# Sixteen batches of graph attention and a routed expert layer on one core: the attention's instruction order on all four engines laid out anew

## Chip, cores and metric

One core of one Trainium2 chip runs the whole program. The metric is the device time in microseconds (us), the median of the runs shown. Engines: PE (TensorE), DVE (VectorE), ACT (ScalarE), POOL (GpSimd), SP (the DMA queue).

## What is computed

The input holds 16 batches of 256 tokens with 128 features. In each batch and each of 16 heads of 64 features:

```python
sim = einsum(q, k) * scale, causal mask;  attn = softmax(sim)
out = attn @ v
adj = clip(attn + eye, 0, 1);  deg = sum(adj)
feats = v
for l in range(2):
    h = feats @ gnn_w[l] + gnn_b[l]
    feats = gelu(adj @ h / deg + feats)
out = layer_norm((out + feats @ lin_w + lin_b) @ Wo)
x = x + out
# then a mixture of 8 experts, two for each token
logits = rmsnorm(layer_norm(x)) @ router;  top 2;  silu(gate) * up @ down
```

## The kernel before

Heads go in 8 pairs n (0 to 7), pairs in 4 doubles d. `queries_keys(b, n)` makes q and k of a pair with three float32r products each, `scores(b, n)` the 256x256 scores of two heads, `maxima` (DVE) and `exps` (ACT) their softmax numerator, `adjacency` (DVE) adds the diagonal and sums a row (`den`), `weights` takes its reciprocal, `graph` (POOL) scales the matrix, `transposes` (PE) turns it and `graph` (ACT) keeps it in SBUF as `gt0`, `gt1`. `differences` (PE) multiplies it by v into the half bank MIX, `degrees` (POOL, then PE) puts den/ssum, transposed, into the half DEG. `difference` (DVE) writes MIX - v to `dT`, `attended` multiplies it by DEG into `aT`. `mixed_values`, `layer1`, `layer2_in` and `layer2` are the graph layers of a double; `layer1_out` and `layer2_out` (DVE) and `gelu1` and `gelu2` (ACT) close them. `output_start`, `output_graph` and `output_attended` add up the output product of a batch in bank 7, `output_natural` turns it.

A tensor instruction uses one of three shapes of the array. Most are 128 rows by 128 columns. `scores` has 64 x 128 (two heads in two row halves). `differences` and `layer2` have 128 x 64 (two heads in two column halves). In the profile they stand as 128\*128, 64\*128 and 128\*64. A block is one call of such a function; a stretch of blocks with one shape is called a group below, and the passage from one group to the next a switch.

The four engines each run a list of calls written out by hand, `batch(b, before, routed, after)`: batches 0 and 1, then a loop over 2 to 14, then batch 15. The list mixes four batches: the attention of b, the rest of the output and norms of b-1, routing of b-2 (`logits`, `places`, `choose`, `place_tokens`, on POOL four `scatter` DMAs), and norm, values and first queries of b+1. Engines meet by counters: `Signal.wait(engine, turn, k)`. Each of the eight PSUM banks has fixed uses (`SCORE_BANKS`, `TURNED_BANKS`, bank 0 for `queries_keys` and `layer1`, 3 and 4 for `transposes`, 5 for MIX and DEG). Behind the batches stands the sorted stage: 71 steps of 128 routed rows, each loaded by DMA, multiplied and stored by an indirect DMA (`rows_out`).

Of the kernel before, what the change touches and what calls it, by code (L numbers as in the profile page):

```python
# [20 lines left out]
P = 128  # L21
BATCHES, TOKENS, DIM = 16, 256, 128
HEADS, DHEAD = 16, 64
# [42 lines left out]
class Signal:  # L66
# [5 lines left out]
    def wait(self, engine, turn, k):  # L72

        engine.wait_ge(self.sem, turn * self.per + k)


def build_program(nc, x, wq, wk, wv, wvT, gnn_w, gnn_b, lin_wT, lin_b, wo, gamma_in, gamma_out,
# [10 lines left out]
    with ctx:  # L88
# [10 lines left out]
        hold = sb("hold", [P, 2])  # L99
# [97 lines left out]
        dT = at("dT", [P, TOKENS])  # L197
# [68 lines left out]
        s_vt, a_vt = Signal(sem("s_vt"), 4), Signal(sem("a_vt"), 4)  # L266
        a_d = Signal(sem("a_d"), PAIRS)
# [47 lines left out]
        LOGITS, PLACES = slice(0, TILES * EXPERTS), slice(0, (SIDE + 1) * EXPERTS)  # L315
# [7 lines left out]
        VALUE_BANKS = (3, 4, 5, 3)  # L323
        L1_BANK, L2_IN_BANKS, L2_BANKS = 0, (2, 2, 2, 4), (1, 1, 1, 3)
        MIX, DEG = slice(0, TOKENS), slice(TOKENS, 2 * TOKENS)

        def score_bank(n, a):
            return bank[SCORE_BANKS[(2 * n + a) % 3]]

# [126 lines left out]
        def _(pool):  # L456
# [71 lines left out]
            def degrees(b, n):  # L528

                s = n % 3  # L530
                if n >= 3:
                    s_deg.wait(pool, b, n - 2)
# [9 lines left out]
            def scatter(p, c):  # L542

                nc.gpsimd.indirect_dma_start(slots, bass.IndirectOffsetOnAxis(ap=row_now[:, c:c + 1], axis=0),
                                             z4[:, c, :], None).then_inc(z_free.sem, 16)

# [16 lines left out]
            def batch(b, before, routed, after):  # L563

                if routed is not None:
                    gate_up_low(b - 1)
                graph(b, 0)
                graph(b, 1)
                degrees(b, 0)
                degrees(b, 1)  # L570
                graph(b, 2)
                degrees(b, 2)
                graph(b, 3)
                graph(b, 4)
                if after is not None:
                    deviation(after, 0, 3)
                if before is not None:
                    token_power(before, 0)
                degrees(b, 3)
                degrees(b, 4)  # L580
                if routed is not None:
                    d_pl.wait(pool, routed, 5)
                graph(b, 5)
                if routed is not None:
                    for c in range(SIDE):
                        scatter(routed, c)
                degrees(b, 5)
                graph(b, 6)
                degrees(b, 6)
                graph(b, 7)  # L590
                degrees(b, 7)
                if after is not None:
                    deviation(after, 1, 7)
                if before is not None:
                    token_power(before, 1)
# [11 lines left out]
            batch(0, None, None, 1)  # L607
            p_deg.wait(pool, 0, PAIRS)
# [36 lines left out]
        def _(pe):  # L645
# [30 lines left out]
            def x_transposed(b, earlier):  # L676
                d_ln.wait(pe, b, 8)
                if earlier is not None:
                    a_exp.wait(pe, earlier, 2 * PAIRS - 1)
                for t in range(TILES):  # L680
                    mm = nc.tensor.transpose(bank[6][:, xt(t)], xh[:, t, :], ident[:, :])
                mm.then_inc(s_xt.sem, 1)

            def values(b, c, earlier):

                t, h = c % 2, c // 2
                if c == 0:
                    a_xt.wait(pe, b, 1)
                    d_xt.wait(pe, b, 1)
                    if earlier is None:  # L690
                        pe.wait_ge(k_vlow, 2)
                    else:
                        a_gt.wait(pe, earlier, PAIRS)
                        d_z2.wait(pe, earlier, DOUBLES)
                if c == 1 and earlier is not None:
                    a_gt.wait(pe, earlier, PAIRS)
                    a_g1.wait(pe, earlier, DOUBLES)
                if c == 2 and earlier is not None:
                    a_d.wait(pe, earlier, PAIRS)
                if c == 3:  # L700
                    a_v.wait(pe, b, 1)
                cols = slice(h * 512, (h + 1) * 512)
                product3(bank[VALUE_BANKS[c]][:, :], xt_hi[:, xt(t)], xt_lo[:, xt(t)],
                         v_hi[:, cols], v_lo[:, cols]).then_inc(s_v.sem, 1)

            def queries_keys(b, n, earlier=None):
                if n == 0:
                    if earlier is not None:
                        d_z1.wait(pe, earlier, DOUBLES)
                    a_xt.wait(pe, b, 1)  # L710
                    d_xt.wait(pe, b, 1)
                else:
                    a_qk.wait(pe, b, n)
                cols = slice(n * P, (n + 1) * P)
                product3(bank[0][:, 0:TOKENS], w_hi[:, 0, cols], w_lo[:, 0, cols], xt_hi[:, :], xt_lo[:, :])
                product3(bank[0][:, TOKENS:], w_hi[:, 1, cols], w_lo[:, 1, cols],
                         xt_hi[:, :], xt_lo[:, :]).then_inc(s_qk.sem, 1)

            def scores(b, n, before=None, routed=None):

                a_qk.wait(pe, b, n + 1)
                if n == 0 and before is not None:
                    d_z2.wait(pe, before, DOUBLES)
                    a_g1.wait(pe, before, DOUBLES)
                if n == 1 and routed is not None:
                    d_ch.wait(pe, routed, 1)
                if n >= 1:
                    a_exp.wait(pe, b, 2 * n - 1)
                q, k = qk[:, n % 2, 0:TOKENS], qk[:, n % 2, TOKENS:]
                for h in range(2):  # L730
                    for a in range(2):
                        rows = slice(a * DHEAD, (a + 1) * DHEAD)
                        diagonal = score_bank(n, a)[:, :].rearrange("p (t j) -> p t j", t=TILES)
# [9 lines left out]
            def values_transposed(b, i):  # L743

                a_v.wait(pe, b, (2, 3, 4, 4)[i])
                if i == 3:
                    a_vt.wait(pe, b, 1)
                o = bank[TURNED_BANKS[i]]
# [7 lines left out]
            def transposes(b, n):  # L756
# [3 lines left out]
                if n >= 1:  # L760
                    a_gt.wait(pe, b, n)
                else:
                    a_vt.wait(pe, b, 4)
                for a in range(2):
                    nc.tensor.transpose(bank[3][:, a * TOKENS:a * TOKENS + P], ea[:, s, a, :], ident[:, :])  # L765
                    nc.tensor.transpose(bank[3][:, a * TOKENS + P:(a + 1) * TOKENS], eb[:, s, a, 0:P], ident[:, :])  # L766
                for a in range(2):
                    mm = nc.tensor.transpose(bank[4][:, a * P:(a + 1) * P], eb[:, s, a, P:], ident[:, :])  # L768
# [11 lines left out]
            def differences(b, n):  # L780

                a_gt.wait(pe, b, n + 1)
                if n >= 1:
                    a_d.wait(pe, b, n)
                mixed(bank[5][:, MIX], lambda t, a: vnat[:, t, n * P + a * DHEAD:n * P + (a + 1) * DHEAD], n)

            def degrees(b, n):

                p_deg.wait(pe, b, n + 1)
                for t in range(TILES):  # L790
                    mm = nc.tensor.transpose(  # L791
                        bank[5][:, DEG][:, xt(t)],
# [3 lines left out]
            def output_natural(b):  # L796

                d_yT.wait(pe, b, 1)
                for t in range(TILES):
                    mm = nc.tensor.transpose(bank[7][:, xt(t)], yT[:, xt(t)], ident[:, :])  # L800
                mm.then_inc(s_yn.sem, 1)

            def layer1(b, d):
# [3 lines left out]
                if d == 0:  # L807
                    a_qk.wait(pe, b, PAIRS)
                else:
# [1283 lines left out]
```

## Time and profile before

| | |
|---|---|
| median of 3 runs | 1095.57 us (1093.75 to 1097.4) |
| profiled execution, span | 1095.5 us |
| PE busy | 1058.7 us, 97% |
| DVE busy | 861.7 us, 79% |
| ACT busy | 783.5 us, 72% |
| POOL busy | 503.4 us, 46% |
| mean granted PE clock | 0.998 |
| chain that ended last | PE 62%, DVE 26%, issue 5%, ACT 2%, DMA 2% |

The profiled execution has no time of its own beside its span of 1095.5 us; it lies 0.1 us from the median. Times are from the span's start. PE busy is a modelled number: matmuls are pipelined, so an engine that reads 97% busy can still lose time between one matmul's start and the next. In the timeline a row merges neighbouring instructions, the second number is its length, and starts can be compared from row to row.

### The profile page before, as it was taken

Reading aid. Unit: us, or ns where it says so; the run is one execution under the profiler, and the core shown is the slowest. Engines: PE = TensorE matmul, PEld = TensorE weight load, DVE = VectorE, ACT = ScalarE, POOL = GpSimd, SP = SyncE. Lnnn points to the kernel's source line nnn. Section 1 sums busy time; section 2 is a strip of 40 time slices with the busy share of each in tenths; the row PEclk is TensorE's granted clock in tenths of the full one; section 3 lists DMA queues with packets and bytes.
Section 4 is the critical chain, followed back from the end, with each engine's and each line's share of the span. In section 5 each row is a group of like instructions: output and inputs, shape, how many; then the busy total and the mean of one; then the engine's idle time right before and its main releaser. Section 6 shows DMA issues by size and latency. Waiting matters only on the chain.

```text
span 1095.5 us, 28320 instructions
## 1 busy us (share of the span) xinstructions
PE 1058.7 (97%) x8600; PEld 857.1 (78%) x8600; DVE 861.7 (79%) x3622; ACT 783.5 (72%) x2180; POOL 503.4 (46%) x654
## 2 busy tenths in 40 slices
PE   5999999999999999999999999999999989999997
PEld 4777777777777777777777777778787767999995
DVE  5758797979798888979797979797979696767554
ACT  5768686868686868686878777778687776656653
POOL 4515254544545453536363626272727251655443
PEclk9999999999999999999999999999999999999999
DMA  6990000000000000000000000000000012222227
GB/s 179 404 328 2 9 2 19 0 18 0 11 7 10 8 10 8 10 8 10 8 10 8 10 8 10 8 10 8 10 8 10 1 38 73 62 65 74 62 60 243
DMA packets 48965, 50.04 MB, mean 46 GB/s; under 512 B 20601, under 2 KB 39291, under 8 KB 48912
## 3 DMA queue, kind: packets, MB, share of 16 engines
q1 hardware_dynamic: 44592, 40.91, 12.2%
q0 software_dynamic: 4320, 8.47, 2.3%
q8 instruction: 28, 0.46, 0.2%
q14 instruction: 25, 0.20, 0.1%
HBM read 21.23 MB, written 28.58 MB: 45 GB/s over the span
## 4 chain that ended last, share of the span: by engine, by line
PE 62%; DVE 26%; issue 5%; ACT 2%; DMA 2%; SPq 2%; POOL 0%; DVEq 0%; POOLq 0%
PE bank L648 51%; DVE eb L1478 6%; DVE nmax L1463 6%; DVE ea L1475 3%; PE bank L791 2%; PE bank L1023 2%; DVE dT L1492 1%; PE bank L765 1%; PE bank L752 1%; PE bank L766 1%; PE bank L768 1%; DVE aT L1497 1%; ACT f1T L1186 1%; DVE z L1512 1%; DMA pairs<-zout,zin 1%
## 5 line engine op out<-in xcount | busy, mean ns | idle before, releaser
L522 POOL TENSOR_TENSOR ea<-ea,wgt 128x256 f32<-128x256 f32 x128 | 78.3, 611 | 308.9 <-DVE wgt L1487 289.3
L1463 DVE TENSOR_REDUCE nmax<-bank 128x1 f32<-128x128 f32 (+1 forms) x512 | 149.3, 346 | 67.0 <-PE bank L648 67.0
L1128 ACT ACTIVATE gt<-bank 128x512 f32<-128x512 f32 (+1 forms) x256 | 111.8, 494 | 41.0 <-PE bank L768 40.2
L1160 ACT ACTIVATE ea<-bank,nmax 128x128 f32<-128x128 f32 x256 | 96.5, 377 | 52.2 <-DVE nmax L1463 29.5
L524 POOL TENSOR_TENSOR eb<-eb,wgt 128x512 f32<-128x512 f32 x128 | 132.7, 1037 | 0.0
L1478 DVE SCALAR_TENSOR_TENSOR eb<-idw,ssum,eb 128x256 f32<-128x256 f32 x256 | 126.2, 530 | 0.0
L1160 ACT ACTIVATE eb<-bank,nmax 128x256 f32<-128x256 f32 x256 | 123.8, 484 | 0.0
L648 PE MATMUL bank<-gt,vnat 128*64 128x256 f32 (+1 forms) x1024 | 111.2, 336 | 11.3 <-ACT gvT L1128 10.5
L648 PEld LDWEIGHTS bank<-gt,vnat 128*64 128x64 f32 x1024 | 68.3, 136 | 56.8 <-issue 35.4
L648 PE MATMUL bank<-qk 64*128 64x128 f32 (+1 forms) x1024 | 112.7, 340 | 0.0
L550 POOL DMA_INDIRECT pairs<-zout,zin x71 | 70.7, 996 | 80.7 <-DVE zout L1983 68.0
L648 PE MATMUL bank<-gt,g 128*64 128x256 f32 (+1 forms) x1024 | 97.0, 330 | 1.0
L648 PE MATMUL bank<-xt_lo,w_hi 128*128 128x256 f32 x256 | 88.3, 345 | 2.3 <-DVE xt_lo L1456 1.9
L648 PEld LDWEIGHTS bank<-gt,g 128*64 128x64 f32 x1024 | 68.5, 137 | 27.3 <-issue 9.5
L1128 ACT ACTIVATE qk<-bank 128x512 f32<-128x512 f32 x128 | 76.8, 600 | 15.3 <-PE bank L648 15.3
L540 POOL TENSOR_TENSOR rs<-ve,half 128x2 f32<-128x2 f32 x48 | 34.4, 716 | 113.1 <-DVE ve L1742 58.8
L533 POOL TENSOR_TENSOR deg<-den,rs 128x256 f32<-128x256 f32 x128 | 82.3, 652 | 0.3
L1186 ACT ACTIVATE f1T<-z,gb 128x512 f32<-128x512 f32 x64 | 46.2, 722 | 48.1 <-DVE z L1512 47.9
L1520 DVE TENSOR_TENSOR z<-bank,f1T 128x512 f32<-128x512 f32 x64 | 44.0, 688 | 46.4 <-PE bank L648 46.3
L1475 DVE SCALAR_TENSOR_TENSOR ea<-ident,ssum,ea 128x128 f32<-128x128 f32 x256 | 79.3, 347 | 0.0
L648 PE MATMUL bank<-aT,wo_sb 128*128 128x256 f32 x256 | 78.1, 388 | 0.0
L1976 DVE TENSOR_TENSOR shid<-bank,ssg 128x352 f32<-128x352 f32 x71 | 37.3, 525 | 50.9 <-ACT ssg L1323 43.4
(240 smaller groups left out, 3102.4 us busy)
## 6 DMA issues: line engine op xcount, KB each, us to landing
slots<-gu_lo SPq DMA_DIRECT2D x33, 520.0 KB, 14.9
zin<-slots SPq DMA_DIRECT2D x71, 65.0 KB, 1.8
got<-pairs SPq DMA_DIRECT2D x8, 512.0 KB, 6.8
zin<-in_guT SPq DMA_DIRECT2D x14, 216.0 KB, 2.9
raw_gu<-in_guT SPq DMA_DIRECT2D x8, 352.0 KB, 4.0
out<-x_all SPq DMA_DIRECT2D x7, 256.0 KB, 3.0
pairs<-zout,zin POOLq DMA_INDIRECT x71, 2.6
dn<-in_downT SPq DMA_DIRECT2D x2, 512.0 KB, 15.6
```

What stands on the lines that cost most here:

```text
L522: nc.gpsimd.tensor_tensor(ea[:, s], ea[:, s], wgt[:, s, 0:2].unsqueeze(2).to_broadcast([P, 2, P]), ALU.mult)
L524: nc.gpsimd.tensor_tensor(eb[:, s], eb[:, s], wgt[:, s, 2:4].unsqueeze(2).to_broadcast([P, 2, 2 * P]), ALU.mult).then_inc(p_g.sem, 1)
L533: nc.gpsimd.tensor_tensor(deg[:, s], den[:, s, :].unsqueeze(2).to_broadcast([P, 4, DHEAD]), rs[:, s, :].unsqueeze(2).to_broadcast([P, 4, D ...
L550: nc.gpsimd.indirect_dma_start(pairs, bass.IndirectOffsetOnAxis(ap=zin[:, j % RING, ID:ID + 1].bitcast(u32), axis=0), zout[:, j % RING, :] ...
L648: return nc_mm(o, st, mo, start=first, stop=last, **more)
L1128: return nc.scalar.activation(o, i, ACT.Copy, **more)
L1160: done = nc.scalar.activation(e[:, s, a, :], score_bank(n, a)[:, TILE_SCORES[t]], ACT.Exp, bias=nmax[:, s, i:i + 1], accum_out=ssum[:, s, ...
L1186: nc.scalar.activation(f1T[:, d % 2, :], z1[:, d % 2, :], ACT.Gelu, bias=gb[:, 0:1]).then_inc(a_f1.sem, 1)
L1463: done = V.tensor_reduce(nmax[:, n % 3, i:i + 1], score_bank(n, a)[:, TILE_SCORES[t]], X, ALU.max, negate=True)
L1475: V.scalar_tensor_tensor(ea[:, s, a, :], ident[:, :], ssum[:, s, a:a + 1], ea[:, s, a, :], ALU.mult, ALU.max, accum_out=den[:, s, a:a + 1])
L1478: done = V.scalar_tensor_tensor(eb[:, s, a, :], idw[:, :], ssum[:, s, 2 + a:3 + a], eb[:, s, a, :], ALU.mult, ALU.max, accum_out=den[:, s, ...
L1520: V.tensor_tensor(z2[:, d % 2, :], bank[L2_BANKS[d]][:, :], f1T[:, d % 2, :], ALU.add).then_inc(d_z2.sem, 1)
```

## The change

Nothing of the computation changes. All four lists are written in another order. On PE: `scores` of pairs 0 and 1, 2 and 3, 4 and 5 stand together, `differences` 2 and 3 too, `differences` 6 behind `layer2(0)`, `layer2` 2 and 3 together. Every use of PSUM has its bank from a table, so that neighbouring blocks write different banks. Waits inside the functions are gone where the order of the lists or one wait in `batch` covers them. `difference` writes `MIX - v` straight to `aT` and `attended` multiplies `aT` in place; `difference` waits for `differences` alone (new signal `s_d`), no longer for `degrees`. One product, `output_attended(b, 3)`, moves to the next batch. On POOL the four scatters move from the middle of the list to its end.

```diff
-        SCORE_BANKS = (1, 2, 6)
-        TURNED_BANKS = (4, 5, 3, 4)
+        SCORE_BANKS = ((1, 5), (4, 6), (3, 2), (0, 5), (3, 0), (5, 4), (6, 5), (6, 3))
+        QK_AT = ((3, 0), (3, 0), (2, 0), (0, 0), (4, 0), (0, 0), (1, 0), (4, 0))
...
             def difference(b, n):
 
-                s_deg.wait(dve, b, n + 1)
-                V.tensor_tensor(dT[:, :], bank[5][:, MIX], vT[:, n, :], ALU.subtract).then_inc(d_d.sem, 1)
+                s_d.wait(dve, b, n + 1)
+                V.tensor_tensor(aT[:, n, :], psum(MIX_AT[n], TOKENS), vT[:, n, :], ALU.subtract).then_inc(d_d.sem, 1)
 
             def attended(b, n):
 
                 d_d.wait(dve, b, n + 1)
-                V.tensor_tensor(aT[:, n, :], bank[5][:, DEG], dT[:, :], ALU.mult).then_inc(d_a.sem, 1)
+                V.tensor_tensor(aT[:, n, :], psum(DEG_AT[n], TOKENS), aT[:, n, :], ALU.mult).then_inc(d_a.sem, 1)
...
             def adjacency(b, n):
 
                 s = n % 3
                 a_exp.wait(dve, b, 2 * n + 2)
-                if n >= 3:
-                    p_deg.wait(dve, b, n - 2)
...
 # POOL, batch()
+                if before is not None:
+                    token_power(b - 1, 0)
+                if routed is not None:
+                    scatters(b - 2)
+                if before is not None:
+                    token_power(b - 1, 1)
                 if routed is not None:
                     z_free.wait(pool, routed, z_free.per)
                 if before is not None:
-                    token_power(before, 2)
+                    token_power(b - 1, 2)
...
 # PE, batch(), beginning and end
-                scores(b, 0, before)
-                queries_keys(b, 2)
-                if routed is not None:
-                    logits(routed, bank[6])
-                values(b, 1, before)
-                values(b, 2, before)
-                scores(b, 1, None, routed)
+                a_v.wait(pe, b, 1)
+                scores(b, 0)
+                d_z2.wait(pe, b - 1, 3)
+                scores(b, 1)
+                a_zt.wait(pe, b - 2, 1)
+                queries_keys(b, 2)
...
+                a_exp.wait(pe, b, 5)
+                values_transposed(b, 0)
+                transposes(b, 0)
...
+                layer2_in(b, 3)
+                layer2(b, 2)
+                layer2(b, 3)
                 output_graph(b, 2)
-                layer2(b, 2)
-                layer2_in(b, 3)
-                if after is not None:
-                    queries_keys(after, 0, b)
-                if before is not None:
-                    tokens_transposed(before, bank[6], after)
-                layer2(b, 3)
...
 # DVE, batch(), middle
                 maxima(b, 5, 1)
+                p_deg.wait(dve, b, 2)
                 adjacency(b, 4)
-                difference(b, 1)
-                weights(b, 4)
+                if before is not None:
+                    output_bias(b - 1)
...
+                difference(b, 1)
+                maxima(b, 6, 0)
+                weights(b, 4)
+                p_deg.wait(dve, b, 3)
+                adjacency(b, 5)
+                maxima(b, 6, 1)
```

The beginning of the loop's list on PE, before. `mask,pick` and `qk` are `scores`, `xt_lo,w_hi` to `xt_hi,w_hi` are `queries_keys`.

```order
L648 MATMUL bank<-mask,pick 128x2x64 x4
L648 MATMUL bank<-qk 128x128 x2
L648 MATMUL bank<-qk 128x256 x2
L74 REGISTER_ALU
L648 MATMUL bank<-xt_lo,w_hi 128x256
L648 MATMUL bank<-xt_hi,w_lo 128x256
```

The same place in the changed kernel.

```order
L665 MATMUL bank<-mask,pick 128x2x64 x4
L665 MATMUL bank<-qk 128x128 x2
L665 MATMUL bank<-qk 128x256 x2
L76 ISA
L76 REGISTER_ALU
L665 MATMUL bank<-mask,pick 128x2x64 x4
L665 MATMUL bank<-qk 128x128 x2
L665 MATMUL bank<-qk 128x256 x2
L665 MATMUL bank<-xt_lo,w_hi 128x256
```

The scores of pair 1 now follow those of pair 0 directly; before, fourteen matmul calls on the full array stood between them.

The end of the loop's list on PE, before, from `tokens_transposed` on (`gt,g` is `layer2`, `f2T,lwo` is `output_graph`).

```order
L970 MATMUL bank<-ident,z 128x128 x2
L648 MATMUL bank<-gt,g 64x256 x2
L648 MATMUL bank<-gt,g 64x128 x2
L648 MATMUL bank<-gt,g 64x256 x2
L648 MATMUL bank<-gt,g 64x128 x2
L74 REGISTER_ALU
L648 MATMUL bank<-xt_lo,w_hi 128x256
```

And in the changed kernel, from `layer2_in(b, 3)` (`gw,f1T`) on.

```order
L665 MATMUL bank<-gw,f1T 128x128 x4
L665 MATMUL bank<-gt,g 64x256 x2
L665 MATMUL bank<-gt,g 64x128 x2
L665 MATMUL bank<-gt,g 64x256 x2
L665 MATMUL bank<-gt,g 64x128 x2
L665 MATMUL bank<-gt,g 64x256 x2
L665 MATMUL bank<-gt,g 64x128 x2
L665 MATMUL bank<-gt,g 64x256 x2
L665 MATMUL bank<-gt,g 64x128 x2
L665 MATMUL bank<-f2T,lwo 128x256
L76 ISA
L974 MATMUL bank<-ident,z 128x128 x2
```

`layer2` of the last two doubles is now one group, and the queries and values of the next batch stand ahead of it.

The loop's list on POOL around the scatters (`slots<-z,row_now`), before.

```order
L522 TENSOR_TENSOR ea<-ea,wgt 128x256
L524 TENSOR_TENSOR eb<-eb,wgt 128x512
L544 DMA slots<-z,row_now 33792x130 x4
L533 TENSOR_TENSOR deg<-den,rs 128x256
L74 REGISTER_ALU
```

And in the changed kernel, at the list's end (`rs<-ve,half` is `token_power`).

```order
L544 TENSOR_TENSOR deg<-den,rs 128x256
L76 ISA
L551 TENSOR_TENSOR rs<-ve,half 128x2
L76 ISA
L561 TENSOR_TENSOR hold<-half 128x1
L555 DMA slots<-z,row_now 33792x130 x4
L76 REGISTER_ALU
L551 TENSOR_TENSOR rs<-ve,half 128x2
```

The scatters now stand behind all eight `graph` and `degrees` of the batch and ahead of two `token_power`.

## Rows read from the trace of the kernel before

**Rows 1.** Page, part 1 (busy) and one group of part 5 (copies of ACT).

```profile
PE 1058.7 (97%) x8600; PEld 857.1 (78%) x8600; DVE 861.7 (79%) x3622; ACT 783.5 (72%) x2180; POOL 503.4 (46%) x654
...
L1128 ACT ACTIVATE qk<-bank 128x512 f32<-128x512 f32 x128 | 76.8, 600 | 15.3 <-PE bank L648 15.3
```

**Rows 2.** Busy time of one loop batch: window, length, PE, PEld, DVE, ACT, POOL, clock, DMA.

```profile
458.10:514.37 56.27, 55.41 (x465) 43.59 (x463) 47.52 (x212) 42.51 (x122) 26.53 (x34) 1.00 0.03 9
```

**Rows 3.** Timeline of PE: start, length, instructions; `transposes` of x for the next batch.

```profile
458.10 0.44 PE L681 MATMUL bank<-ident,xh 128*128 128x128 f32 x2
...
514.37 0.44 PE L681 MATMUL bank<-ident,xh 128*128 128x128 f32 x2
```

**Rows 4.** Timeline of PE in that batch, blocks inside a group and beside a switch.

```profile
495.86 0.38 PE L791 MATMUL bank<-ident,deg 128*128 128x128 f32 x2
496.07 0.27 PE L765 MATMUL bank<-ident,ea 128*128 128x128 f32 x1
...
496.73 0.60 PE L648 MATMUL bank<-aT,wo_sb 128*128 128x256 f32 x2
...
500.68 0.27 PE L765 MATMUL bank<-ident,ea 128*128 128x128 f32 x1
...
501.43 0.87 PE L648 MATMUL bank<-gt,vnat 128*64 128x256 f32 x8
502.23 0.44 PE L791 MATMUL bank<-ident,deg 128*128 128x128 f32 x2
502.51 1.03 PE L648 MATMUL bank<-gvT,gw 128*128 128x256 f32 x4
...
504.60 0.87 PE L648 MATMUL bank<-gt,vnat 128*64 128x256 f32 x8 [0.17 <-ACT gvT L1128]
505.27 1.50 PE L648 MATMUL bank<-gt,g 128*64 128x256 f32 x16
```

**Rows 5.** Timeline of PE, `differences(2)` and what it waited for.

```profile
494.59 0.87 PE L648 MATMUL bank<-gt,vnat 128*64 128x256 f32 x8 [0.38 <-ACT gvT L1128]
```

**Rows 6.** Timeline of PE, start of a batch: `scores(0)`, `queries_keys(2)`, `logits`, then `values(1)`.

```profile
469.12 0.29 PE L648 MATMUL bank<-mask,pick 64*128 64x128 bf16 x4
...
470.05 0.38 PE L648 MATMUL bank<-xt_lo,w_hi 128*128 128x256 f32 x1
...
470.84 0.51 PE L648 MATMUL bank<-rtT,zT 128*128 128x8 f32 x4
471.20 0.48 PE L648 MATMUL bank<-v_lo,xt_hi 128*128 128x512 f32 x1
```

**Rows 7.** Timeline of ACT, `exps(3, 0)` and the start of `exps(3, 1)`.

```profile
482.90 0.38 ACT L1160 ACTIVATE ea<-bank,nmax 128x128 f32<-128x128 f32 x1
...
483.71 0.38 ACT L1160 ACTIVATE ea<-bank,nmax 128x128 f32<-128x128 f32 x1
```

**Rows 8.** Timeline of POOL, first scatter of a batch, what follows the fourth, and one `token_power`.

```profile
500.51 1.06 POOL L544 DMA_INDIRECT slots<-z,row_now  x1 [0.17 <-issue]
...
505.56 0.73 POOL L533 TENSOR_TENSOR deg<-den,rs 128x256 f32<-128x256 f32 x1
...
514.87 0.69 POOL L540 TENSOR_TENSOR rs<-ve,half 128x2 f32<-128x2 f32 x1 [3.35 <-DVE ve L1692]
```

**Rows 9.** Timeline of DVE, one instruction of `adjacency` at two places.

```profile
484.68 0.48 DVE L1478 SCALAR_TENSOR_TENSOR eb<-idw,ssum,eb 128x256 f32<-128x256 f32 x1
...
900.20 1.82 DVE L1478 SCALAR_TENSOR_TENSOR eb<-idw,ssum,eb 128x256 f32<-128x256 f32 x1
```

**Rows 10.** Timeline of POOL beside the last of them.

```profile
900.71 1.03 POOL L524 TENSOR_TENSOR eb<-eb,wgt 128x512 f32<-128x512 f32 x1
```

**Rows 11.** Timeline of PE, `tokens_transposed` in loop and last batch, last `transposes` of x.

```profile
465.33 0.38 PE L970 MATMUL bank<-ident,z 128*128 128x128 f32 x2
...
851.96 0.44 PE L681 MATMUL bank<-ident,xh 128*128 128x128 f32 x2
...
920.29 0.44 PE L970 MATMUL bank<-ident,z 128*128 128x128 f32 x2 [0.38 <-DVE z L1752]
```

More of the change, by code:

```diff
@@ L918, in batch @@
-                degrees(b, 2)
-                transposes(b, 4)
-                output_attended(b, 0)
-                scores(b, 7)
-                differences(b, 3)
-                degrees(b, 3)
-                layer1(b, 0)
-                output_attended(b, 1)
+                    output_attended(b - 1, 6)
+                a_exp.wait(pe, b, 9)
+                transposes(b, 2)
+                a_qk.wait(pe, b, 7)
+                degrees(b, 1)
+                if before is not None:
+                    output_attended(b - 1, 7)
+                    output_graph(b - 1, 7)
@@ new lines, in batch @@
+                degrees(b, 2)
+                degrees(b, 3)
+                differences(b, 2)
+                differences(b, 3)
+                d_y.wait(pe, b - 1, 1)
+                scores(b, 7)
+                a_d.wait(pe, b, 2)
+                transposes(b, 4)
+                output_attended(b, 1)
+                output_attended(b, 2)
+                a_exp.wait(pe, b, 14)
+                layer1(b, 0)
+                a_gt.wait(pe, b, 5)
+                degrees(b, 4)
+                values_transposed(b, 2)
@@ L939, in batch @@
-                degrees(b, 6)
-                transposes(b, 7)
+                degrees(b, 7)
+                if after is not None:
+                    x_transposed(b + 1)
+                differences(b, 7)
+                d_z1.wait(pe, b, 3)
                 layer2(b, 1)
-                differences(b, 7)
                 if after is not None:
-                    x_transposed(after, b)
-                degrees(b, 7)
+                    a_d.wait(pe, b, 7)
+                    queries_keys(b + 1, 0)
@@ L946, in batch @@
                 output_graph(b, 0)
+                layer1(b, 3)
+                layer2_in(b, 2)
+                if after is not None:
+                    a_qk.wait(pe, b + 1, 1)
+                    queries_keys(b + 1, 1)
+                    d_z2.wait(pe, b, 2)
+                    values(b + 1, 0)
                 output_graph(b, 1)
-                output_attended(b, 3)
-                layer2_in(b, 2)
-                layer1(b, 3)
+                layer2_in(b, 3)
+                layer2(b, 2)
@@ new lines, in batch @@
+                weights(b, 6)
+                if before is not None:
+                    norm_tokens(b - 1, 0)
+                a_vt.wait(dve, b, 3)
+                difference(b, 4)
+                layer1_out(b, 1)
+                attended(b, 4)
+                adjacency(b, 7)
+                if routed is not None:
+                    choose(b - 2, 2)
+                weights(b, 7)
+                difference(b, 5)
+                if routed is not None:
+                    place_tokens(b - 2, 0)
@@ L1593, in batch @@
+                attended(b, 5)
+                layer2_out(b, 0)
+                difference(b, 6)
+                if before is not None:
+                    norm_tokens(b - 1, 1)
+                attended(b, 6)
+                if after is not None:
+                    norm_step(b + 1, 5)
+                if routed is not None:
+                    place_tokens(b - 2, 1)
+                layer1_out(b, 2)
                 if after is None:
                     table_first(0)
+                if before is not None:
+                    norm_tokens(b - 1, 2)
@@ L1608, in batch @@
[L1608 to L1616 removed]
+                    x_low(b + 1)
+                if before is not None:
+                    norm_tokens(b - 1, 3)
+                attended(b, 7)
```

554 lines of the change are left out of this document (246 added, 308 removed).

## The prediction

> **What bounds the kernel now.** I read the busy shares first. PE is busy for 97% of the span, DVE for 79%, ACT for 72%, POOL for 46% [rows 1]. Only something that makes PE's own list shorter can give much. Next comes the window of one loop batch, from one `transposes` of x to the next, 514.37 - 458.10 = 56.27 us [rows 3]. In it PE is busy 55.41 us, so its idle time is 0.86 us, while DVE has 47.52 and ACT 42.51 [rows 2]. Sixteen such batches are some 900 us of the span; the sorted stage behind them is not touched.
>
> Then I ask what the busy time consists of, and here the length of a row says less than the distance between starts. The same block takes different times by what stands beside it [rows 4]. `transposes` with full-array work on both sides takes 496.73 - 496.07 = 0.66 us; with `differences` behind it, which uses 128\*64, it takes 501.43 - 500.68 = 0.75. `differences` takes 502.23 - 501.43 = 0.80 us when the full array comes next, but 505.27 - 504.60 = 0.67 when `layer2` follows, which has its own shape. `degrees` takes 0.21 us (495.86 to 496.07) behind full-array work and 502.51 - 502.23 = 0.28 behind `differences`. So PE loses time where the array's shape changes: 0.09 or 0.13 us at the end of the block before, and 0.07 at the start of the block behind.
>
> **The change, part by part.**
>
> *Switches.* I counted the groups in the two lists for a loop batch. Before there are 33 switches: each of the 8 `scores` and most of the 8 `differences` and 4 `layer2` stand alone. In the changed list there are 21. Scores 0 and 1, 2 and 3, 4 and 5 take away two each, differences 2 and 3, differences 6 behind `layer2(0)`, and `layer2` 2 and 3 two each: 12. By the rows of the last paragraph one switch costs between 0.09 (nothing at the entry) and 0.20 us (0.13 + 0.07). I take 0.14: the exit of 0.09 plus a part of the entry, since the entry is seen on small blocks and large ones may hide it. That is 12 x 0.14 = 1.68 us in each batch, with 1.1 and 2.4 as ends. It lies wholly on PE, which nothing hides.
>
> *Waits of PE.* The loop batch has 0.86 us of idle time [rows 2]. One part is `differences(2)`, which waited 0.38 us for the one MIX bank to be copied by `mixed_values(1)` [rows 5]. With banks from tables this cause is gone. What comes next? I checked the new order at three places by adding up blocks.
>
> At the beginning, PE reaches `values_transposed(0)` after 4 scores, 3 `queries_keys`, `logits`, a `values` and four products of the output. `scores` is 0.93 us, `queries_keys` 0.79, `logits` 0.36 [rows 6]; with some 0.8 for `values` and 0.4 for each output product (estimates: as many columns as `queries_keys`, and half of it) this is 3.7 + 2.4 + 0.4 + 0.8 + 1.7 = 9.0 us, less 0.2 for the switches gone, 8.8 us. It now waits for `exps(2, 0)`. On ACT five `exps` at 483.71 - 482.90 = 0.81 us [rows 7] and three copies of 0.6 [rows 1] stand ahead of its end, 5.9 us, and they can begin when the first scores (0.93 us) and their `maxima` (some 0.6 us, an estimate) are through: 7.4 us. About 1.4 us are left, which waits on the way may use up.
>
> At the end, POOL has the four scatters ahead of the last two `token_power`. They take 505.56 - 500.51 = 5.05 us, a `token_power` 0.69 [rows 8]. DVE's `norm_tokens(7)` waits for the second power and `norm_tokens(11)` for the third, and `layer2_out(2)` and `layer2_out(3)` are queued behind them. From `place_tokens(1)` on this chain is 5.05 + 0.7, then four norm steps and a power, about 2.6, then two more DVE steps of about 0.7 each: 9.8 us. In the same time PE has from `x_transposed` to the next batch's second scores 13 us of work by the same block sums: 4 blocks of `layer2` of 1.4 us and half, two `queries_keys`, `values`, two `layer2_in`, `layer1`, three output products, the first scores. Some 3 us of cover: I cost the move of the scatters at nothing. If the cover were gone, `scores(1)` would be late first.
>
> In the middle the matter is DVE. At 47.5 us of work in 54.6 it is 87% used, against 84% before, and between `adjacency(2)` and `layer1_out(0)` it hardly rests. `attended(2)` must be through before PE's `output_attended(2)`, and `layer1_out(0)` before `degrees(5)`. My additions leave next to no slack there. So I don't count the 0.38 us as won, nor any of the 0.86: I put the idle time after equal to that before. The ends are 0 (a gain of 0.9) and 2.5 us.
>
> *In place and fewer waits.* `difference` and `attended` stay two DVE instructions of the same size; one reads SBUF where it read `dT`, nothing gained. `difference` can begin before `degrees`: this only gives DVE freedom. The counters that go are checks without work; PE's list has fewer, and I cost them at nothing: where a count had long been reached, the rows show the next block starting without a gap. `output_attended(b, 3)` is only moved. Batches 0, 1 and 15 use the same lists, so the switches go there too.
>
> *Batch 15.* In the loop `tokens_transposed` starts 465.33 - 458.10 = 7.2 us after a window opens [rows 3, 11]. The last of those windows opens at 851.96, so it would end 56.27 us later at 908.23, and the start would be at 908.23 + 7.2 = 915.5; it was at 920.29, 4.8 us late [rows 3, 11], although PE has fewer blocks there. Eight `gate_up_high` on ACT and `table_first` on DVE stand in the way. The new list spreads them singly; it may give 3 us or take 2. I leave it at 0.
>
> **Sum.** The profiled span is 1095.5 us, 0.1 from the median of 1095.57, so it can stand for it. 16 x 1.68 = 26.9 us: 1095.5 - 26.9 = 1068.6, **1069 us**. A batch should take 54.6 us.
>
> **The other ways.**
>
> *Waits shrink too.* If the spread banks remove nearly all idle time and a switch is worth more than 0.14, a batch is 53.7 us: 16 x 2.6 = 41, giving 1054. For it: the waits now are for single banks [rows 5]. Against: DVE's load in the middle.
>
> *DVE and POOL in each other's way, part of the gain lost.* An `adjacency` instruction of 0.48 us took 1.82 us at 900.20 [rows 9], while POOL ran its `graph` instruction from 900.71 on [rows 10]. The two were in each other's way. The Trainium skill, SBUF — State Buffer, section Who interferes with whom, says that a VectorE instruction with two inputs in SBUF contends with a GpSimd instruction that reads SBUF; the trace agrees at this place. In the new order `adjacency` 4 to 7 fall in the stretches in which POOL does `graph` and two `degrees` in a row, since these now follow each other without scatters between. If half of the 16 large and small instructions of these four are held for 0.3 us, the middle is 2.4 us later than in my sum, and after the little slack some 1 us of it stays as waits of PE: 16 x (1.68 - 1) = 11, giving 1085.
>
> *The same, and slower than before.* All 16 held, some by 1.3 us as at 900.20, is 16 x 0.3 + 1.3 = 6 us of delay a batch, of which 3 us can't be caught up: the batch is 54.6 + 3.0 = 57.6 us and the time 1095.5 + 16 x 1.3 = 1116. The place is `output_attended(2)`, `layer1(0)` and `degrees(5)` on PE; the point from which it decides is 1.7 us more waiting in a batch than now, since PE is the bound and never wins back what it waited.
>
> *The saving is not there.* The price of a switch might be a drain that has to come anyway before the next block's results are used, then 12 fewer change nothing: 1095. Against it: 0.67 and 0.80 us for the same eight instructions.
>
> **Chances.** Forecast 1069 with its neighbours (1062 to 1078): 0.5. Waits shrink: 0.18. Part lost, about 1085: 0.17. No saving: 0.05. Slower, about 1116: 0.10. A measurement of this kernel can tell 0.3%, some 3 us, from no change. Faster is then 0.5 + 0.18 + 0.16 = 0.84, within 0.3% 0.05, slower 0.11. The range reaches from 1054, the better end of the waits, to 1088, the partial loss with its spread, and leaves out some 2 in 10.
>
> **What would show it.** The distance between two starts of `transposes` of x in the loop: 54.6 us; 53.7 or 55.6 for the two neighbours. 21 switches in a batch; a block of `scores` that follows another starts some 0.1 us sooner behind it than 0.93. PE's idle time in the window near 0.9 us. If the batch is longer than 55.5, the waits list must name DVE (`aT`, `z`) or ACT behind DVE as releaser, and `adjacency` instructions of more than 0.5 us must be many in the middle. If `layer2_out(2)` is late behind `norm_tokens(7)`, the scatters were not covered. The forecast is wrong in its ground if the loop batch has 12 switches fewer and is not shorter although PE doesn't wait.

## The result, and the profile after

The changed kernel takes 1054.45 us, the median of four runs between 1054.06 and 1054.87. The kernel before took 1096.49 beside it, the median of four runs between 1093.75 and 1098.01. The ratio is 0.9623, with a 95% interval from 0.9607 to 0.9638: faster by 42 us, where 27 was forecast. That is the lower end of the range, and the time that the rival "waits shrink too" gave (1054, with a loop batch of 53.7 us; it came out at 53.5).

The page of the changed kernel, whose profiled span is 1053.1 us; the first line is its part 1, to be held against [rows 1], the second its part 4, the shares of the chain of waits that ended last.

```profile
PE 1022.9 (97%) x8600; PEld 855.3 (81%) x8600; DVE 856.3 (81%) x3622; ACT 777.8 (74%) x2180; POOL 505.3 (48%) x668
...
PE 78%; DVE 11%; ACT 3%; issue 3%; DMA 2%; SPq 2%; POOL 0%; POOLq 0%; DVEq 0%; ACTq 0%
```

PE is still busy for 97% of the span, and the span is 42.4 us shorter: what became shorter is PE's own busy time. The window of one loop batch, between two `transposes` of x (us of the window, then the busy time and instructions of PE, PE's weight loads, DVE, ACT and POOL, then the granted clock):

```profile
544.66:598.14 53.48, 53.12 (x465) 43.52 (x464) 47.23 (x210) 42.07 (x122) 26.59 (x35) 1.00 0.03 9
```

Against [rows 2] the window went from 56.27 to 53.48 us and PE's busy time from 55.41 to 53.12, with the same 465 matmul records. Counted in the traces from the array shape of each record, a batch has 21 switches where it had 33. Idle time is 0.36 where it was 0.86. All the waiting of PE that the rows show is now in one place, at `scores(7)`. Rows of PE's timeline (start, length, engine, line, operation):

```profile
544.65 0.38 PE L696 MATMUL bank<-ident,xh 128*128 128x128 f32 x2
...
556.91 0.28 PE L665 MATMUL bank<-mask,pick 64*128 64x128 bf16 x4
...
557.74 0.28 PE L665 MATMUL bank<-mask,pick 64*128 64x128 bf16 x4
...
583.34 0.29 PE L665 MATMUL bank<-mask,pick 64*128 64x128 bf16 x4 [0.36 <-DVE y_now L1502]
...
598.13 0.38 PE L696 MATMUL bank<-ident,xh 128*128 128x128 f32 x2
```

The reader is to see two things. `scores(1)` starts 557.74 - 556.91 = 0.83 us behind `scores(0)`, where a block of scores that had the full array behind it took 0.93 [rows 6]. And `scores(7)` waits for `y_now`, which `output_kept` on DVE copies out of the bank in which the scores go. By the starts on either side this wait is 0.43 us (0.36 in the row), so a batch that doesn't wait there would take 53.48 - 0.43 = 53.04 us (unrounded starts). That number is the yardstick below.

Where the 42.4 us of the two spans came from, by the starts of `transposes` of x: the start -0.1 (its end came 0.1 later); batch 0 0.3 (55.55 to 55.28); batch 1 3.5 (55.99 to 52.53); thirteen batches of 2.79, 36.3; batch 15 2.6; the sorted stage nothing (172.9 and 173.0). For batch 15, the first row is the first product of the sorted stage in the kernel before, the others are the end of batch 15 in the changed one.

```profile
922.64 0.27 PE L1005 MATMUL bank<-ident,zin 128*128 128x128 f32 x1
```

```profile
875.01 1.16 PE L665 MATMUL bank<-gw,f1T 128*128 128x128 f32 x8 [1.56 <-ACT f1T L1182]
...
879.46 0.38 PE L974 MATMUL bank<-ident,z 128*128 128x128 f32 x2
...
880.12 0.27 PE L1007 MATMUL bank<-ident,zin 128*128 128x128 f32 x1
```

From the last `transposes` of x (851.96 [rows 11], and 812.03 now) to this product it is 70.68 us before and 68.09 now, although a wait of 1.56 us for ACT stands in it.

The contention that the prediction feared is there. DVE's timeline around `adjacency(5)`, and POOL's for the same stretch:

```profile
472.48 0.31 DVE L1472 SCALAR_TENSOR_TENSOR ea<-ident,ssum,ea 128x128 f32<-128x128 f32 x1
...
472.73 0.69 DVE L1472 SCALAR_TENSOR_TENSOR ea<-ident,ssum,ea 128x128 f32<-128x128 f32 x1
...
473.35 1.25 DVE L1475 SCALAR_TENSOR_TENSOR eb<-idw,ssum,eb 128x256 f32<-128x256 f32 x1
...
474.53 0.82 DVE L1475 SCALAR_TENSOR_TENSOR eb<-idw,ssum,eb 128x256 f32<-128x256 f32 x1
...
475.82 0.41 DVE L1502 COPY y_now<-bank 128x256 f32<-128x256 f32 x1
```

```profile
472.57 0.70 POOL L535 TENSOR_TENSOR ea<-ea,wgt 128x256 f32<-128x256 f32 x1 [2.39 <-DVE wgt L1484]
473.23 1.09 POOL L537 TENSOR_TENSOR eb<-eb,wgt 128x512 f32<-128x512 f32 x1
474.28 0.79 POOL L544 TENSOR_TENSOR deg<-den,rs 128x256 f32<-128x256 f32 x1
```

`weights(4)` on DVE releases POOL's `graph(4)` and `degrees(4)` just as DVE begins `adjacency(5)`. The large instruction that takes 0.48 us alone [rows 9] takes 1.25 and 0.82 here, and the block is through after 2.9 us. In a whole batch 6 of the 32 instructions of `adjacency` are longer than their like (2 before), and this block has 3 of them. `y_now`, the copy for which PE waits, comes right behind it.

The scatters' move. POOL's rows and DVE's at the end of a batch:

```profile
491.59 1.06 POOL L555 DMA_INDIRECT slots<-z,row_now  x1 [0.16 <-issue]
...
496.45 0.73 POOL L551 TENSOR_TENSOR rs<-ve,half 128x2 f32<-128x2 f32 x1
```

```profile
497.22 0.60 DVE L1697 TENSOR_SCALAR t<-x_all,mv,rs 128x128 f32 x2 [0.65 <-POOL rs L551]
...
499.72 0.61 DVE L1748 TENSOR_SCALAR z<-t,rs 128x256 f32<-128x256 f32 x2 [0.80 <-POOL rs L551]
...
500.96 0.69 DVE L1513 TENSOR_TENSOR z<-bank,f1T 128x512 f32<-128x512 f32 x1 [0.48 <-PE bank L665]
```

DVE does wait for the powers behind the scatters, 0.65 and 0.80 us, and then `layer2_out(2)` still has to wait 0.48 us for PE. The move is covered.

### The profile page after: what moved, and what is told of

Read it like the earlier page. It is cut to its first block, busy times and chain, and to the rows that moved or that the text cites. A ratio compares the mean times of both kernels' runs of the same rounds, so it can differ in the third digit from the quotient of the medians.

```text
span 1053.1 us, 27818 instructions
## 1 busy us (share of the span) xinstructions
PE 1022.9 (97%) x8600; PEld 855.3 (81%) x8600; DVE 856.3 (81%) x3622; ACT 777.8 (74%) x2180; POOL 505.3 (48%) x668
## 4 chain that ended last, share of the span: by engine, by line
PE 78%; DVE 11%; ACT 3%; issue 3%; DMA 2%; SPq 2%; POOL 0%; POOLq 0%; DVEq 0%; ACTq 0%
PE bank L665 65%; DVE eb L1475 4%; DVE ea L1472 3%; PE bank L742 2%; PE bank L752 2%; PE bank L1025 2%; PE bank L753 2%; PE bank L755 2%; DVE nmax L1462 2%; PE bank L777 2%; ACT ea L1159 1%; ACT eb L1159 1%; DMA pairs<-zout,zin 1%; PE bank L1007 1%; DVE y_now L1502 1%
## 5 line engine op out<-in xcount | busy, mean ns | idle before, releaser
L1475 DVE SCALAR_TENSOR_TENSOR eb<-idw,ssum,eb 128x256 f32<-128x256 f32 x256 | 136.9, 570 | 0.0
L665 PE MATMUL bank<-gt,vnat 128*64 128x256 f32 (+1 forms) x1024 | 107.2, 335 | 0.4 <-ACT gt L1129 0.4
L665 PE MATMUL bank<-gt,g 128*64 128x256 f32 (+1 forms) x1024 | 92.2, 327 | 0.3 <-ACT g L1129 0.3
L665 PEld LDWEIGHTS bank<-gt,vnat 128*64 128x64 f32 x1024 | 63.2, 136 | 35.6 <-issue 16.0
L1129 ACT ACTIVATE gvT<-bank 128x256 f32<-128x256 f32 x128 | 49.9, 390 | 55.8 <-DVE aT L1494 55.7
L1472 DVE SCALAR_TENSOR_TENSOR ea<-ident,ssum,ea 128x128 f32<-128x128 f32 x256 | 90.9, 391 | 0.0
L665 PEld LDWEIGHTS bank<-gt,g 128*64 128x64 f32 x1024 | 65.4, 137 | 21.0 <-ACT g L1129 0.7
L665 PE MATMUL bank<-f2T,lwo 128*128 128x256 f32 x256 | 77.7, 386 | 0.3 <-ACT f2T L1192 0.3
L665 PE MATMUL bank<-aT,wo_sb 128*128 128x256 f32 x256 | 73.7, 391 | 0.0
L665 PE MATMUL bank<-xt_hi,w_hi 128*128 128x256 f32 x256 | 72.5, 283 | 0.0
```

Of the source, the lines that this page charges most:

```text
L665: return nc_mm(o, st, mo, start=first, stop=last, **more)
L1129: return nc.scalar.activation(o, i, ACT.Copy, **more)
L1472: V.scalar_tensor_tensor(ea[:, s, a, :], ident[:, :], ssum[:, s, a:a + 1], ea[:, s, a, :], ALU.mult, ALU.max, accum_out=den[:, s, a:a + 1])
L1475: done = V.scalar_tensor_tensor(eb[:, s, a, :], idw[:, :], ssum[:, s, 2 + a:3 + a], eb[:, s, a, :], ALU.mult, ALU.max, accum_out=den[:, s, ...
```

## The experiments

Two theories at the start: the gain is the price of the switches (A), or it comes mostly from shorter waits that the new order and its banks allow (B). Three kernels put switches back without moving anything far: one puts back six, one two, and a control makes a neighbour's move of the same kind without a switch more.

**Six switches back.** On PE:

```diff
                 scores(b, 2)
-                scores(b, 3)
                 if before is not None:
                     output_attended(b - 1, 3)
+                scores(b, 3)
+                if before is not None:
                     output_attended(b - 1, 4)
...
                 scores(b, 4)
-                a_gt.wait(pe, b, 2)
-                scores(b, 5)
                 if before is not None:
                     output_attended(b - 1, 5)
+                a_gt.wait(pe, b, 2)
+                scores(b, 5)
...
                 degrees(b, 2)
-                degrees(b, 3)
                 differences(b, 2)
+                degrees(b, 3)
                 differences(b, 3)
```

> The changed kernel with one full-array block set back between scores 2 and 3, between scores 4 and 5 and between differences 2 and 3: 27 switches in a loop batch where it has 21, the same blocks otherwise. Theory A (a switch costs PE 0.14 to 0.20 us): the loop batch goes from 53.5 to 54.3 to 54.7 us, the whole by 13 to 19 us. Theory B (the gain came from shorter waits alone, a switch costs nothing): 53.5 us, no change.

It took 1063.77 us (1062.34 to 1065.66), ratio 0.9701 [0.9682, 0.9720] to the kernel before. PE's timeline:

```profile
549.58 0.38 PE L696 MATMUL bank<-ident,xh 128*128 128x128 f32 x2
...
588.78 0.29 PE L665 MATMUL bank<-mask,pick 64*128 64x128 bf16 x4
...
603.58 0.38 PE L696 MATMUL bank<-ident,xh 128*128 128x128 f32 x2
```

A batch has 27 switches and takes 54.00 us, and `scores(7)` (the middle row) shows no wait: PE comes later, so `y_now` is there. Six switches therefore cost 54.00 - 53.04 = 0.96 us at most, 0.16 each; by the starts 0.05 of it is still waiting at `scores(7)`, which leaves 0.15 each. The saved wait hides some 0.4 of it. That put the batch under the 54.3 to 54.7 that A had named.

**Two switches back.** The second of the three hunks alone, `output_attended(5)` between scores 4 and 5.

```diff
                 scores(b, 4)
-                a_gt.wait(pe, b, 2)
-                scores(b, 5)
                 if before is not None:
                     output_attended(b - 1, 5)
+                a_gt.wait(pe, b, 2)
+                scores(b, 5)
```

> Only the block between scores 4 and 5 is set back: 23 switches. Theory A: one third of what the six cost, 0.28 to 0.40 us in a batch (53.75 to 53.87). Theory B: 53.47, no change.

**The control.** `output_attended(5)` behind `queries_keys(6)` instead; 21 switches as before.

```diff
                 scores(b, 5)
+                queries_keys(b, 6)
                 if before is not None:
                     output_attended(b - 1, 5)
-                queries_keys(b, 6)
```

> The same product as in the run with two more switches is moved past queries_keys(6), inside its group: 21 switches as before. Theory A: 53.5 us within 0.1. If it moves by more, then the moved product and not the switch explains part of the run with two.

The waits at `scores(7)`, first with two switches more, then the control:

```profile
586.11 0.29 PE L665 MATMUL bank<-mask,pick 64*128 64x128 bf16 x4 [0.28 <-DVE y_now L1502]
```

```profile
582.02 0.29 PE L665 MATMUL bank<-mask,pick 64*128 64x128 bf16 x4 [0.21 <-DVE y_now L1502]
```

With two switches more the batch takes 53.70 us with 0.34 of waiting by the starts, so 53.35 without: 0.31 above 53.04 (unrounded), 0.155 for a switch. The control takes 53.32 with 0.28 of waiting, again 53.04 without. One run each took 1059.42 and 1055.89 us. The control's batch is 0.16 us shorter than the changed kernel's, outside the 0.1 that was expected, and all of that is waiting. So this move of a block costs nothing by itself, and a switch costs 0.15 to 0.16 us at these places.

**All switches and all waits, by the starts.** The switches put back are not the twelve that the change took away, so their price can't simply be multiplied by 12. The traces settle it. Rows of PE in the kernel before, to be read with [rows 4] and [rows 5]:

```profile
486.30 0.70 PE L648 MATMUL bank<-aT,wo_sb 128*128 128x256 f32 x2
486.84 0.38 PE L791 MATMUL bank<-ident,deg 128*128 128x128 f32 x2
...
497.26 0.28 PE L648 MATMUL bank<-mask,pick 64*128 64x128 bf16 x4
...
500.25 0.60 PE L648 MATMUL bank<-aT,wo_sb 128*128 128x256 f32 x2
...
506.70 0.44 PE L791 MATMUL bank<-ident,deg 128*128 128x128 f32 x2
507.26 1.16 PE L648 MATMUL bank<-gw,f1T 128*128 128x128 f32 x8
```

`output_attended` takes 500.68 - 500.25 = 0.43 us with no switch beside it, 497.26 - 496.73 = 0.53 ahead of one and 486.84 - 486.30 = 0.54 behind one. Read so for every block, from the starts of its single matmuls, the exit costs 0.09 to 0.10 us (0.07 once) whatever the block. The entry costs 0.10 in the full-array products, 0.06 in transposes, 0.05 in `differences` and `layer2`, and 0.01 in `scores`. Summed over one loop batch, 33 switches are 4.9 us before and 21 are 3.2 now: the twelve that went are worth 1.68 us, 0.14 each. The six put back come to 0.91 by the same prices, 0.15 each.

The same starts give the waits. Before there are 1.7 us of them in a batch: 0.45 and 0.24 at the two `differences` that wait for the MIX bank, 0.38 at `layer1` behind `degrees` (507.26 - 506.70 = 0.56 where 0.28 is usual beside a switch [rows 4], and its first product is 0.1 late), and four of 0.11 to 0.24. All of these are gone. Two new ones have come, 0.43 at `scores(7)` and 0.15 at `transposes(7)`, together 0.58. That is 1.1 us less waiting, and 1.7 + 1.1 make up the 2.79. So theory A holds for 60% of the gain and theory B for 40%.

**One MIX bank's wait back.** To see what the tables of banks are worth for MIX, `differences(n)` waits again until `mixed_values(n - 1)` has copied, as with the single bank of before. On PE:

```diff
+                if n >= 1:
+                    a_d.wait(pe, b, n)
```

> The changed kernel with the old wait of a single MIX bank put back: differences(n) waits until mixed_values(n-1) has copied its half bank; order and banks stay. Theory A (the spread banks took the waits away, so putting the wait back brings back what the old kernel waited): the loop batch grows by 0.4 to 0.9 us. Theory B (the new order alone would have kept the wait short): below 0.1 us.

Both theories were far off. It took 1207.54 us (1205.71 to 1208.75), ratio 1.1021 [1.1000, 1.1041]. Window and PE's rows:

```profile
510.10:573.40 63.30, 55.61 (x464) 45.01 (x463) 47.11 (x209) 42.16 (x122) 26.75 (x36) 0.95 0.03 8
```

```profile
551.14 1.55 PE L665 MATMUL bank<-gt,vnat 128*64 128x256 f32 x8 [2.57 <-ACT gvT L1131]
554.42 1.55 PE L665 MATMUL bank<-gt,vnat 128*64 128x256 f32 x8 [1.73 <-ACT gvT L1131]
```

This batch is 63.3 us, 9.8 more than 53.48 (batches of 62.7 and 63.4 us take turns). A wait of one block cost 0.38 us in the old order, where other blocks stood between two differences [rows 5]. With them side by side it is a round trip from PE over DVE to ACT and back, 2.57 us at the longest, five waits and 7.7 us in a batch. The granted clock in the window is 0.95 where it was 1.00, with this much idle time, and PE's busy time is 55.61 us where it was 53.12. So for MIX the banks are not a gain beside the order: the new order can't be had without them. The other banks of the tables were not tried one by one.

**The differences not in place.** The tile `dT` comes back, and with it the wait that one tile needs:

```diff
+                if n >= 1:
+                    d_a.wait(dve, b, n)
-                V.tensor_tensor(aT[:, n, :], psum(MIX_AT[n], TOKENS), vT[:, n, :], ALU.subtract).then_inc(d_d.sem, 1)
+                V.tensor_tensor(dT[:, :], psum(MIX_AT[n], TOKENS), vT[:, n, :], ALU.subtract).then_inc(d_d.sem, 1)
...
-                V.tensor_tensor(aT[:, n, :], psum(DEG_AT[n], TOKENS), aT[:, n, :], ALU.mult).then_inc(d_a.sem, 1)
+                V.tensor_tensor(aT[:, n, :], psum(DEG_AT[n], TOKENS), dT[:, :], ALU.mult).then_inc(d_a.sem, 1)
```

> The changed kernel with differences written to their own tile dT again and, since one tile serves all pairs, DVE waiting for attended(n-1) before difference(n). Theory A (in place is worth nothing by itself, the sizes are the same and the wait is for an instruction that DVE has long done): the batch stays within 0.1 us of 53.47. Theory B (the wait of DVE on itself costs in the middle, where DVE has no slack): it grows by 0.2 to 0.5 us.

The batch is 53.57 us, 0.10 more, and one run took 1058.28. That difference of the totals is near what one run can tell, but the period of the batch is the same from batch to batch within 0.02, so the 0.10 stands; by the starts it is waiting at `transposes(7)`, where 0.15 had stood already. Computing in place is worth next to nothing, as costed.

**Is there slack on DVE in the middle?** The four reductions of `maxima(4)` are done twice, the second time into a spare tile: 1.06 us more on DVE.

```diff
+                if n in TWICE:
+                    for t in range(TILES):
+                        at_ = 4 * (n - 4) + 2 * t + a
+                        V.tensor_reduce(spare[:, at_:at_ + 1], score_bank(n, a)[:, TILE_SCORES[t]], X, ALU.max)
```

> The changed kernel with the four reductions of maxima(4) done twice, the copies into a spare tile: 1.06 us more work for DVE ahead of the middle of a batch. Theory A (as the prediction had it, DVE has next to no slack there): the batch grows by 0.8 to 1.1 us. Theory B (the new order has slack): below 0.4 us.

```profile
498.54 0.38 PE L698 MATMUL bank<-ident,xh 128*128 128x128 f32 x2
...
538.12 0.29 PE L667 MATMUL bank<-mask,pick 64*128 64x128 bf16 x4 [0.88 <-DVE y_now L1508]
...
552.93 0.38 PE L698 MATMUL bank<-ident,xh 128*128 128x128 f32 x2
```

The batch takes 54.39 us, 0.91 more for 1.06 us added, and one run took 1070.09. The wait at `scores(7)` (the middle row) grew by 0.5, and by the starts PE now also waits 0.3 to 0.4 at `output_start`, which needs `yT` from DVE. In the middle of a batch, work of DVE is on the path, although DVE is busy in only 47 of 53 us.

**What covers the scatters?** Four powers into a spare tile stand ahead of them on POOL.

```diff
+                for c in range(3, 7):
+                    nc.gpsimd.tensor_tensor(hold[:, c:c + 1], inv_e[:, 0:1], inv_e[:, 1:2], ALU.pow)
```

> The changed kernel with four powers of one column, some 2.8 us in all, ahead of the four scatters on POOL. Theory A (the prediction's block sums: 3 us of PE work cover the scatters): the batch stays within 0.2 us. Theory B (norm_tokens(7) and (11) already wait 0.65 and 0.80 us for POOL and layer2_out(2) stands behind them, so the cover is near 1.5 us): the batch grows by 1.0 to 1.5 us.

```profile
546.96 2.16 POOL L563 TENSOR_TENSOR hold<-inv_e 128x1 f32<-128x1 f32 x4
```

2.16 us more on POOL cost 0.31 us in a batch (53.78), one run 1061.30. That lies between the two theories. The slack behind the scatters was thus some 1.85 us (an estimate: 2.16 less 0.31), not the 3 of the prediction, and not nothing. By the starts PE becomes late at `values(1)` and `values(2)`, not at `scores(1)`, where the prediction looked for it.

**Taking the last wait away, first way.** On DVE `output_kept` is put ahead of `maxima(6, 1)`; on PE the control's move is kept.

```diff
                 adjacency(b, 5)
-                maxima(b, 6, 1)
                 if before is not None:
                     output_kept(b - 1, psum(Y_NOW_AT, TOKENS))
+                maxima(b, 6, 1)
```

> The changed kernel with output_kept of the batch before put ahead of maxima(6, 1) on DVE, and output_attended(5) behind queries_keys(6) on PE. scores(7) waits 0.43 us in each batch for output_kept. Theory A (this is the one wait that PE has left in a loop batch, and nothing else becomes late): the batch goes from 53.47 to 53.04 us and the whole by some 6 us, to about 1048. Theory B (exps(6, 1), now 0.33 us later, or another chain is late instead): 53.3 or more.

1050.19 us (1049.79 to 1052.45), ratio 0.9586 [0.9569, 0.9603], batch 53.21. The wait for `y_now` is gone, but the one near the end of the batch, where `transposes(7)` stands behind a wait for DVE's `layer2_out(0)`, has grown from 0.15 to 0.30 us by the starts. Of the 0.43 us, 0.27 were won and the rest was only put off, a result between the two theories.

**Second way: take away the cause.** On DVE `weights(4)` goes behind `adjacency(5)`, so that POOL gets its `graph(4)` when DVE is past those instructions.

```diff
-                weights(b, 4)
...
                 adjacency(b, 5)
+                weights(b, 4)
```

Timed once:

> The changed kernel with weights(4) put behind adjacency(5) on DVE, so that POOL's graph(4) no longer runs beside adjacency(5), which took 2.94 us in place of 1.43. Theory A (it is POOL's reading that holds these instructions): adjacency(5) takes 1.5 us, output_kept comes over 1 us earlier, the wait of scores(7) goes, the batch takes 53.1 us. Theory B (adjacency is long for another reason, or graph(4) is then late for transposes(4)): no shorter than 53.4.

It took 1047.71 us with a batch of 52.98. Then five times:

> The kernel with weights(4) behind adjacency(5) again, now timed against the kernel before over five rounds. From its loop batch of 52.98 us, 0.49 less than the changed kernel's, and some 15 batches: 7 us under the changed kernel's 1054.5, so 1047 to 1048; a ratio to the kernel before of 0.955 to 0.957.

1047.87 us (1046.58 to 1048.49), ratio 0.9555 [0.9542, 0.9568]: **this beats both kernels**, the changed one by 0.6%. PE's, then DVE's rows for `adjacency(5)`, then the group of the large instruction in the whole kernel, which is to be held against the last fence, of the changed kernel:

```profile
487.30 0.38 PE L696 MATMUL bank<-ident,xh 128*128 128x128 f32 x2
...
540.30 0.38 PE L696 MATMUL bank<-ident,xh 128*128 128x128 f32 x2
```

```profile
522.04 0.32 DVE L1472 SCALAR_TENSOR_TENSOR ea<-ident,ssum,ea 128x128 f32<-128x128 f32 x1
...
522.56 0.47 DVE L1475 SCALAR_TENSOR_TENSOR eb<-idw,ssum,eb 128x256 f32<-128x256 f32 x1
...
522.97 0.47 DVE L1475 SCALAR_TENSOR_TENSOR eb<-idw,ssum,eb 128x256 f32<-128x256 f32 x1
...
523.37 0.17 DVE L1484 RECIPROCAL wgt<-den 128x4 f32<-128x4 f32 x1
...
523.97 0.41 DVE L1502 COPY y_now<-bank 128x256 f32<-128x256 f32 x1
```

```profile
L1475 DVE SCALAR_TENSOR_TENSOR eb<-idw,ssum,eb 128x256 f32<-128x256 f32 x256 | 113.9, 481 | 0.0
```

```profile
L1475 DVE SCALAR_TENSOR_TENSOR eb<-idw,ssum,eb 128x256 f32<-128x256 f32 x256 | 136.9, 570 | 0.0
```

The large instructions are back at 0.47 us, and the mean over all 256 fell from 570 to 481 ns. `adjacency(5)` takes 1.3 us where it took 2.9, `y_now` is there in time, and the batch is 53.00 us, at the 53.04 that was worked out for a batch that doesn't wait at `scores(7)`. In the window PE is now busy in all of it; by the starts 0.1 us of waiting is left, at `transposes(7)`. The instructions are the same and as many; only what POOL did beside them was moved. So this wait came from the two engines being in each other's way, and not from too much work on DVE.

## Why the prediction was right and wrong

**The ground was right.** PE was the bound and stayed it; the larger part of the gain is 12 switches fewer in a batch, 33 to 21, and shows in PE's busy time. The sorted stage didn't move.

**The term of the switch was right in size.** "0.14: the exit of 0.09 plus a part of the entry" is what the twelve cost by the starts, 1.68 us in all. The reason given for it, that large blocks may hide the entry, is half right: `scores` hides it (0.01) and `differences` half of it (0.05), but the large products of the full array pay more than the small blocks, 0.10. That these balance to 0.14 is in part luck. The exit of 0.13 that was read from `differences`, 0.80 against 0.67, is too long by 0.03: the block of 0.67 had just waited, and `layer2` behind it took that much longer; the starts of single matmuls give 0.10.

**The step "I put the idle time after equal to that before" failed,** and is the whole miss. The prediction found the cause of the 0.38 us wait [rows 5] and then gave it away again for want of slack. It also took 0.86 us for all the waiting, from the busy time of the window; by the starts it was 1.7, since short waits stand inside the rows and count as busy. All of it went, 0.7 us of it at the MIX bank, and 0.58 came at two new places: 1.1 us less, where the sum had put 0 and the best end of the prediction was 0.9. How this gain divides between the new order and the new banks wasn't tried: the tables of banks without the new order, or the old order with the new banks.

**The lack of slack on DVE was right, its effect not.** The 1.06 us put into `maxima(4)` came out as 0.91. But no slack means that work added to DVE counts, not that new waiting must arise: the new waits are 0.43 us at `scores(7)` and 0.15 at `transposes(7)`, much less than what went elsewhere. At `output_attended(2)`, `layer1(0)` and `degrees(5)`, where the prediction looked for it, there is none.

**The rival of contention was right in mechanism and wrong in size.** Its price was 1 us of PE's waiting a batch for the milder case and 3 for the other; the instructions are slower, one of them 1.25 us instead of 0.48, and PE paid 0.43 of it. The Trainium skill says that a VectorE instruction with two inputs in SBUF contends with a GpSimd instruction that reads SBUF (SBUF — State Buffer, section Who interferes with whom); the experiment that pulls the two apart agrees: 1.25 us beside POOL, 0.47 without. The prediction counted 8 or 16 held instructions; 6 were held, and what mattered was one block, the last before the copy that PE waits for.

**The scatters** were covered, with some 1.85 us, not some 3. The reading was on the right side with less room than it said. The check of the start, `values_transposed(0)` without a wait, and in place at nothing (0.10 us) held.

**The batches outside the loop.** "Batches 0, 1 and 15 use the same lists, so the switches go there too" is right for the switches and not for the time: batch 0 has 11 fewer inside its window and gained 0.3 us, since PE's waits behind its first block rose from 4.2 to 5.6 us in the list of its releasers. Batch 1 gained 3.5 and batch 15, left at 0, 2.6 us, within the +3 that was given as its end.

Altogether: 16 x 1.68 = 27 was forecast. The loop batches' 2.79 is the 1.68 that was forecast for the switches and 1.1 for the waits that were put at nothing. Of the rival "waits shrink too", the waits came true and the dearer switch did not.

## What to carry to other kernels

When PE is the bound and its blocks have several array shapes, count the changes of shape, take the price from blocks of the same work with different neighbours, and put blocks of one shape together. Take the waits from the distances between starts as well: here the rows hid half of them. Grouped blocks need banks of their own: with the wait of a single one they paid a round trip over two engines. Then read which wait is left, and ask of the instruction before the releaser whether it is slow or merely late: here a block that was twice its length, while another engine had just been released to work beside it, was cured by moving one small step by one place.

## What the runs showed of the hardware that was not expected

- A switch of the array's shape costs 0.14 us of PE on the mean of the twelve taken away and 0.15 in the six put back. The exit is nearly the same for every block, 0.09 to 0.10 us; the entry goes from 0.01 (`scores`) over 0.05 (`differences`, `layer2`) to 0.10 us (full-array products).
- Matmul rows hid waiting: in the window before, 0.86 us was idle, and the starts show 1.7 us of waits.
- The granted clock had a mean of 0.95 over a batch in which PE was idle for 7.7 of 63.3 us, so for part of it PE was on the lower of its two levels (1.2 GHz, not 2.4); the other versions, with at most 1.0 us of idle time in a batch, have 1.00.
- DVE's two-input instruction went from 0.48 to 1.25 us beside POOL's, while POOL's large instruction of `graph` was near its mean (1.09 against 1.05 us) and `degrees` took 0.79 against a mean of 0.64: here DVE pays most of it.
